# A one-core layer of windowed attention and routed experts: the end of the routing stage rearranged

## The reference

```
logits = xn @ wg                      # 4096 tokens, 8 experts
top-2 experts per token, gates = softmax of the two
pos = running count of each expert's tokens;  kept if pos < capacity (1024)
disp[e, pos] = xn[token]              # 8 experts x 1024 slots
y = relu(disp @ w1[e] + b1[e]) @ w2[e] + b2[e]
ffn[token] = sum of gate * y[expert, pos] over its two experts
attention: 16 heads of 16, queries in blocks of 64, band of 64 keys back, softmax, @ w_out
```

## Time and profile before

| | |
|---|---|
| three timed runs, median (lowest to highest) | 733.26 us (733.17 to 733.62) |
| the profiled execution | 732.93 us, of which the span from first to last instruction is 731.1 us |
| TensorE busy | 684.1 us, 94% |
| VectorE, ScalarE, GpSimd busy | 449.0, 452.2, 379.2 us |
| granted clock of TensorE, mean over the span | 0.965 |

### The profile page before, as it was taken

One profiled execution on the slowest core, in us unless ns is written; L12 is line 12 of the kernel. 1 busy time (PEld: TensorE's weight loads), 2 busy tenths in 40 slices (PEclk: granted clock), 3 DMA queues, 4 the chain that ended last, 5 costly groups with the idle time before them and its releaser, 6 DMA issues. The chain is left out here.

```text
span 731.1 us, 19852 instructions
## 1 busy us (share of the span) xinstructions
PE 684.1 (94%) x6849; PEld 599.4 (82%) x6849; DVE 449.0 (61%) x1680; ACT 452.2 (62%) x1459; POOL 379.2 (52%) x543
## 2 busy tenths in 40 slices
PE   5654899999999999999999999899999999999987
PEld 3443689899898998989989888788888888898976
DVE  7984343543534425344253441689989898989895
ACT  4552570844807439165292560888979898888892
POOL 4556460543514525246153310578668677588774
PEclk7976799999999999999999999899999999999999
DMA  9734031142222422224223001432436354534332
GB/s 306 271 115 156 27 112 56 65 143 86 91 67 72 136 93 78 80 72 129 60 72 119 23 12 50 132 89 86 116 103 165 84 151 117 143 91 122 109 107 75
DMA packets 59056, 76.44 MB, mean 105 GB/s; under 512 B 9448, under 2 KB 51560, under 8 KB 58984
## 3 DMA queue, kind: packets, MB, share of 16 engines
q1 hardware_dynamic: 52488, 58.69, 25.5%
q0 software_dynamic: 6144, 16.79, 8.1%
q10 hardware_dynamic: 352, 0.04, 0.0%
HBM read 51.81 MB, written 17.03 MB: 94 GB/s over the span
## 5 line engine op out<-in xcount | busy, mean ns | idle before, releaser
L1101 ACT ACTIVATE a_p<-a_p,a_nmax 128x128 f32<-128x128 f32 x512 | 198.1, 392 | 33.0 <-DVE a_nmax L1140 32.5
L750 DVE TENSOR_TENSOR m_hl<-m_hf,m_hh 128x512 fp32r<-128x512 f32 x128 | 93.2, 728 | 100.0 <-ACT m_hh L707 100.0
L66 PE MATMUL m_psY<-m_w2h,m_hh 128*128 128x256 f32 x512 | 145.1, 283 | 0.0
L66 PE MATMUL m_psY<-m_w2l,m_hh 128*128 128x256 f32 x512 | 143.9, 281 | 0.0
L66 PE MATMUL m_psY<-m_w2h,m_hl 128*128 128x256 f32 x512 | 143.8, 281 | 0.0
L703 ACT ACTIVATE m_hf<-m_psF,b1T 128x512 f32<-128x512 f32 x128 | 88.1, 688 | 66.5 <-PE m_psF L66 52.0
L1140 DVE CUSTOM_DVE_ANT_0 a_p<-a_psS,mask 128x128 f32<-128x128 f32 x512 | 117.4, 286 | 15.6 <-PE a_psS L1265 15.0
L671 POOL CAST m_w2h<-raw 128x256 fp32r<-128x256 f32 x64 | 25.9, 405 | 178.2 <-PE m_psY L66 120.6
L66 PE MATMUL m_psF<-m_xh,w1h 128*128 128x512 f32 x256 | 103.6, 405 | 1.9 <-DVE m_xl L727 1.9
L66 PE MATMUL m_psF<-m_xl,w1h 128*128 128x512 f32 x256 | 102.0, 399 | 0.0
L66 PE MATMUL m_psF<-m_xh,w1l 128*128 128x512 f32 x256 | 102.0, 398 | 0.0
(11 more groups left out here) (200 smaller groups left out, 1357.7 us busy)
## 6 DMA issues: line engine op xcount, KB each, us to landing
raw<-in_L_ffn_w SPq DMA_DIRECT2D x16, 1024.0 KB, 5.4
y_scratch<-y SPq DMA_DIRECT2D x64, 128.0 KB, 1.7
n_xin<-in_L_attn_x SPq DMA_DIRECT2D x8, 512.0 KB, 7.8
xn_scratch<-n_xn SPq DMA_DIRECT2D x8, 512.0 KB, 7.0
a_res<-in_L_attn_x SPq DMA_DIRECT2D x8, 512.0 KB, 4.7
a_rall<-recip_scratch SPq DMA_DIRECT2D x31, 128.0 KB
xnr<-xn_scratch SPq DMA_DIRECT2D x7, 512.0 KB, 5.5
out<-a_res SPq DMA_DIRECT2D x7, 512.0 KB, 3.7
```

Source lines behind the costliest of these rows:

```text
L66: last = pe.matmul(out, a, b, start=(n_start and i == 0), stop=(n_stop and i == n - 1))
L750: dve.tensor_tensor(hl[:, u // HC, u % HC, :], hf[:, u % FR, :], hh[:, u // HC, u % HC, :].bitcast(fp32), ALU.subtract).then_inc(hl_done, 1)
L1101: act.activation(e, e, ACT.Exp, scale=-1.0, bias=nmax[:, r, j:j + 1], accum_out=sums[:, r, j:j + 1]).then_inc(exp_done, 1)
```

## The change

Five edits, in `route_phase` and `moe_phase`:

1. POOL makes 3 rows of `ohV` a round instead of 5, ACT 9 instead of 7.
2. PE computes the values of round `g + 1` before it waits for the one-hots of round `g` (the first round's stand before the loop).
3. The first four gathers are issued by POOL within `route_phase`, after a semaphore `tokens` that DVE sets with `token_of`; the tiles `xg` and their semaphores are created outside both blocks for that. The other four stay in `moe_phase`.
4. The load of `xnr` is moved from the start of `moe_phase` to the start of the last expert on SP.
5. SP waits, before it loads the next expert's `w1`, until the first two transposed groups of the current expert are there (`t_done`).

```diff
-        BY_DVE, BY_POOL, BY_ACT = slice(0, 4), range(4, 9), range(9, R)
+        BY_DVE, BY_POOL, BY_ACT = slice(0, 4), range(4, 7), range(7, R)
...
+            pool.wait_ge(m.tokens, 1)
+            for j in range(ST // 2):
+                pool.indirect_dma_start(m.xg[j][:, :], None, xn_dram,
+                                        bass.IndirectOffsetOnAxis(ap=m.token_of[:, j:j + 1], axis=0))\
+                    .then_inc(m.xg_in[j], 16)
...
-            for g in range(C // R):
-
+            def values(g):
                 pe.wait_ge(item_free, 4 + g - 1)
...
+            values(0)
+            for g in range(C // R):
+                if g + 1 < C // R:
+                    values(g + 1)
                 for part in (hot_b, hot_tile, hot_place):
                     pe.wait_ge(part, g + 1)
...
-            link(dve.scalar_tensor_tensor(m.token_of[:, :], tab_ps[:, 0:E * ST], float(P), tabp[:, :],
-                                          ALU.mult, ALU.add))
+            dve.scalar_tensor_tensor(m.token_of[:, :], tab_ps[:, 0:E * ST], float(P), tabp[:, :], ALU.mult, ALU.add)\
+                .then_inc(m.tokens, 1)
...
-            ut = L // 2 // P
-            sp.dma_start(m.xnr[:, :, :], xn_dram.rearrange("(t p) d -> p t d", p=P)[:, ut:2 * ut, :])\
-                .then_inc(xnr_in, 16)
-
...
-                if not last:
-
+                if last:
+                    ut = L // 2 // P
+                    sp.dma_start(m.xnr[:, :, :], xn_dram.rearrange("(t p) d -> p t d", p=P)[:, ut:2 * ut, :])\
+                        .then_inc(xnr_in, 16)
+                else:
+
+                    alone(sp, t_done, e * TG + KD)
...
-                for j in range(ST):
+                for j in range(ST // 2 if first else 0, ST):
```

More of the change, by code:

```diff
@@ L588, in moe_phase @@
         idx = sb("m_idx", [P, ST], u32)
-        xg = [sb(f"m_xg{j}", [P, D], fp32) for j in range(ST)]
+        xg, xg_in = m.xg, m.xg_in
         xh, xl = sb("m_xh", [P, KD, CAP], fp32r), sb("m_xl", [P, KD, CAP], fp32r)
@@ L599, in moe_phase @@
         idx_done = sem("m_idx_done")
-        xg_in = [sem(f"m_xg_in{j}") for j in range(ST)]
         t_done = sem("m_t_done")
@@ L1363, in build @@
             m.w1l = inner.enter_context(nc.sbuf_tensor("w1l", [P, KD, H], fp32r))
+            m.xg = [inner.enter_context(nc.sbuf_tensor(f"xg{j}", [P, D], fp32)) for j in range(ST)]
+            m.xg_in = [inner.enter_context(nc.semaphore(f"xg_in{j}")) for j in range(ST)]
+            m.tokens = inner.enter_context(nc.semaphore("tokens"))
             with ExitStack() as early:
```

## The result

| | before | after |
|---|---|---|
| five timed runs each, median (lowest to highest) | 733.17 us (731.78 to 733.62) | 729.34 us (728.74 to 730.53) |
| the profiled execution, and its span | 732.93 / 731.1 us | 730.53 / 728.6 us |
| first product of expert 0 | 77.46 us | 73.93 us |

The change makes the kernel 3.8 us faster; the ratio is 0.9945, with a 95% interval of 0.9934 to 0.9957. The forecast was 728.0 us in a range of 725.4 to 730.2. The profiled execution of the changed kernel is the slowest of its five, so its span understates the gain.

A forecast was written before the change was run, and what follows sets the result against it. TensorE bounds the experts, so an earlier first product should move the end equally. Routing 2.25, gather 0's start 0.48, landing and transposes 2.49 make 5.22 us: 733.26 - 5.2 = 728.0 us, range 725.4 to 730.2.

The forecast's parts named there:

- Rounds: Routing's rounds: fewer GpSimd rows and values a round ahead start table 3 2.25 us earlier; ends 0 and 2.3.
- Rival (a): Routing's rounds: ScalarE takes GpSimd's place and nothing is gained there; 730.3 us; chance 0.14 with milder forms.
- Gather 0: First gather after `token_of`: begins 0.79 us behind it instead of 1.27 (ends 0.30 and 1.27), a gain of 0.48 us.
- Landing: Gathers ahead of expert 0: gather 3 lands in 2.8 us (ends 2.7 and 6.9); landing and transposes gain 2.49 us.
- The barrier: Between routing and experts: opens 0.49 us behind GpSimd's early issues, transposes from 68.3 us; at worst 70.2, 1.7 us less gain.
- Two terms of the sum: Before expert 0: gather 0's earlier start, 0.48 us, and landing with transposes, 2.49 us, were added as separate gains.
- Second gathers and loads: Expert 0: gathers 4 to 7 meet the `w1` load but land by 80.0 us, needed at 80.3; cost 0, end about 1 us.
- rival (d): Expert 0: the second four gathers, beside 1 MB of `w1`, stop TensorE at its 4th group; 735 us; chance 0.03.
- The clock: Half-clock stretches at expert 0 (5.1 us) and attention's entry (6.8 us) were taken as unchanged, 0 us.
- Gathers beside loads: Second gathers: beside one load a gather should at most double, to 5.6 us; measured 6.9 kept a small chance of slower.

The follow-up runs named there:

- e10: The changed kernel with edit 3 undone, so all eight gathers are behind the barrier again; 729.11 us, ratio 0.9941.
- e7: The changed kernel with the eight transposes of gathers 0 to 3 moved ahead of the barrier, into routing; 727.36 us, ratio 0.9917.
- e5: The changed kernel with 1.5 MB of extra loads issued by SP beside the early gathers, once `token_of` is there; one run, 733.64 us.
- e2: The kernel before with edit 3 alone (first four gathers ahead of the barrier); 731.96 us, ratio 0.9973.
- e4: The changed kernel with edits 4 and 5 undone, so `xnr` and the next `w1` load early again; 729.76 us, ratio 0.9952.
- e3: The kernel before with edits 4 and 5 alone (the two loads begin later); 731.64 us, ratio 0.9972.
- e13: The changed kernel without edit 3, next `w1` held for all four transposed groups, unread products behind the barrier and around the transposes; 727.03 us, ratio 0.9903.
- e12: The changed kernel run again without any edit; 730.10 us, ratio 0.9946.
- e9: The changed kernel with transposes ahead of the barrier, unread products in TensorE's waits, next `w1` held for all four transposed groups; 726.86 us, ratio 0.9899.

## Why the prediction was right, and where it was off

- *Rounds: right.* Table 3 starts at 60.47 us (60.3), with ScalarE as its releaser; `token_of` is there at 62.24 (62.1); the clock is 1.00 from table 0 on, as I chose. Rival (a) is half true: ScalarE is the last of the three, but the rounds still give 2.1 us. Whether the clock holds is less sure than I wrote: in e10, behind the same 1.25 us of idle as in the changed kernel, table 3 ran at half clock. My choice, 1.4 us of idle against a row of 1.7, was no safe ground.
- *Gather 0: right, at the early end of its bounds.* It starts 0.30 us behind `token_of`, and I took 0.79.
- *Landing: right, as far as the traces show it.* 2.7 us for gather 2; for gather 3 at most 2.8 in e7 (65.70 to 68.49). I took 2.8.
- *The barrier: the mis-sized term.* I let it open 0.49 us behind the last issue, at 68.3 us, and named as the worst end that GpSimd's block ends only when the data has landed: 70.2 and 1.7 us less gain. It opened for TensorE at 70.12. Transposes after 70 us because the barrier came late were among my signs that the prediction is wrong: on this step it was. The drain of 7.26 us shows it, e5 moves it with the data, and e7 ends it 0.16 us behind gather 3 and gets 1.5 us back by putting work under it. From there to the first product I had 3.94 us, and it took 3.81. So 1.82 - 0.13 = 1.69 us is all that separates the first product (73.93) from its forecast (72.24). (My 1.7 us for this end was a little low by its own rows: eight transposes at 1.54 us for six, from 70.2, end near 72.25, 1.9 us behind 70.36.)
- *Two terms of the sum are not two gains.* I counted gather 0's earlier start (edit 3) and the quieter landing (edits 4 and 5) as separate gains. Edit 3 alone already puts the gathers ahead of the loads, so the loads' new place adds nothing behind it (e2, e4), and it puts the barrier at the landing, so that the eight transposes, which used to follow the landings one by one, all queue behind it. All three give 1.44 us for the start, less than the 2.27 of edits 4 and 5 alone (e3).
- *Second gathers and loads: right.* No pause, at no cost; rival (d) did not happen, even with both loads beside them (e4).
- *The clock: right in the mean, wrong in the argument.* The first product came 3.5 us earlier and the timed median 3.8. The single profile shows 2.5, because behind the first product it lost 0.3 us in the experts and 0.8 us in the rest; lined up product by product, TensorE falls behind by 0.3 and by 0.4 us within two runs of the products into `a_psO`, 107 and 165 us behind the experts' end, with no wait that the trace names, so the cause stays open. I had held the 0.45 us spread of three runs against a scatter of the stretch at expert 0. The two traces of the changed kernel show that it scatters: 5.9 and 3.1 us. The Trainium skill (TensorE: Matmul & The Clock Gate, The HAM clock gate) says that the number of slow products varies from run to run; the traces agree, with 5.9 and 3.1 us at half clock, and three runs were too few to argue with: five of the same kernel lie 1.8 us apart (731.78 to 733.62).
- *Gathers beside loads: my bound does not hold, and the rule behind it is not tested.* In e5 three gathers took 6.3, 7.6 and 6.9 us, against 3.5, 2.9 and 2.7 in the changed kernel, but 5.1, 4.0 and 3.1 in e4, where no load ran beside them either. The Trainium skill (DMA: Bandwidth & Descriptors, Queues, rings and completion order) has each engine take turns between queues, packet by packet. That a gather beside loads would at most double is my own step: it leaves out that these gathers, 1.25 us apart and longer than that, also stand behind each other in their own queue. The same gap lies in the 6.9 us of the earlier trace rows, so neither it nor e5 speaks for or against the rule.

## What to carry to other kernels

A transfer that is issued early must not be waited for by more than its reader: behind a gather that GpSimd issues at the end of a block, the block's barrier becomes a wait of every engine for the data, so put the reader's work under it, or leave the gather behind the barrier. When two edits aim at one wait, run each alone: here one alone shortened the start by 2.27 us and both together by 1.44. Where an engine idles just before a long stretch that it bounds, ask what clock it comes back with: here 39 products that nobody reads made the experts' stage 1.4 to 2.7 us shorter than in the two profiles of the changed kernel.

## What the runs showed of the hardware

- GpSimd's drain at a block's end ended with the landing of its gathers (e7: 68.65 us, 0.16 us behind TensorE's release by the last of them), while SP's ended in 0.12 us with 1.5 MB of its own in flight (e5).
- A gather that waits for a semaphore within its block started 0.30 us behind the result it waits for; across the barrier 1.27 us (before, e13).
- TensorE's half-clock stretch at attention's entry was 6.8 us in the changed kernel, 10.2 in e12 and 13.7 in e9, whose code there is the same.
- The experts' stage took 374.3 us at full clock, and some 0.45 us more for each us of it at half clock (up to 5.9 us, 376.9).
